# A convolution, attention and LoRA-expert block: stores issued by ScalarE, residual sums fused on VectorE, one pass of the output projection, a new timetable of the side work

## The reference

```python
x = x + layernorm(attn(layernorm(x)))
x = x + layernorm(ffn(layernorm(x)))
# attn: convolution over tokens, 3 taps, 1024 -> 768 (+ bias), split into q, k, v of 256;
#   wq, wk, wv to 16 heads of 64 (+ biases); blocks of 128 tokens: causal softmax(q k / 8) v;
#   wo back to 256 (+ bo); proj_w 256 -> 1024 (+ proj_b)
# ffn: logits = x Wr^T over 4 experts, the best 2, softmax of those as gates;
#   delta = sum_e gate_e * (x A_e^T) B_e^T * 4, rank 16
```

## Time and profile before

| | |
|---|---|
| median of 3 runs | 935.11 us (932.56 to 935.26) |
| the profiled execution, its own time | 938.93 us |
| its span, first to last instruction | 937.1 us |
| mean granted TensorE clock | 0.914 |
| TensorE / VectorE / ScalarE / GpSimd busy | 769.7 / 632.5 / 414.0 / 405.9 us |
| moved by DMA | 160.64 MB |

### The profile page before, as it was taken

How to read it: one execution, slowest core, us unless ns; L and a number is a source line. 1 busy time by engine, 2 the same in 40 slices (tenths; PEclk the granted TensorE clock), 3 DMA queues, 4 the chain that set the end, 5 groups by cost and what they waited for, 6 DMA issues and landing times.

```text
span 937.1 us, 14761 instructions
## 1 busy us (share of the span) xinstructions
PE 769.7 (82%) x5136; PEld 683.4 (73%) x5136; DVE 632.5 (67%) x1742; ACT 414.0 (44%) x1000; POOL 405.9 (43%) x348
## 2 busy tenths in 40 slices
PE   2489858999789788999879788999878877997573
PEld 1488757788679677888779776888778876876472
DVE  5999945995586545986496555886486551655846
ACT  3453345775335325675125325675135323454232
POOL 2566663575564441465164451455164450121111
PEclk9979988999989888999898988999898989999856
DMA  7267793334955475313944565312944444425102
GB/s 216 71 217 237 283 347 138 131 116 137 336 202 203 135 280 197 108 58 115 365 160 169 169 249 205 129 51 99 383 168 169 158 157 170 135 81 185 38 1 90
DMA packets 106361, 160.64 MB, mean 171 GB/s; under 512 B 7600, under 2 KB 76208, under 8 KB 106288
## 3 DMA queue, kind: packets, MB, share of 16 engines
q1 hardware_dynamic: 106288, 159.70, 49.0%
HBM read 128.22 MB, written 31.46 MB: 170 GB/s over the span
## 4 chain that ended last, share of the span: by engine, by line
PE 47%; DVE 28%; DMA 8%; ACT 5%; issue 5%; POOL 4%; SPq 2%; ACTq 0%; DVEq 0%; POOLq 0%
PE bank L763 11%; PE bank L764 10%; PE bank L765 10%; DMA w_pair<-kept_pairs 5%; PE bank L859 4%; PE bank L840 4%; PE bank L897 3%; PE bank L848 2%; ACT prob L1013 2%; DVE stats L1317 2%; PE bank L890 2%; DVE newton L1099 2%; DVE newton L1100 2%; POOL work L1399 2%; DVE ln_r L1097 2%
## 5 line engine op out<-in xcount | busy, mean ns | idle before, releaser
L763 PE MATMUL bank<-f_hi,w_pair 128*128 128x256 f32 x768 | 228.0, 297 | 25.7 <-DVE w_pair L1168 7.3
L764 PE MATMUL bank<-f_lo,w_pair 128*128 128x256 f32 x768 | 222.3, 290 | 0.0
L765 PE MATMUL bank<-f_hi,w_pair 128*128 128x256 f32 x768 | 221.8, 289 | 0.0
L1373 POOL TENSOR_TENSOR w_pair<-raw,w_pair 128x512 fp32r<-128x512 f32 (+1 forms) x115 | 148.7, 1306 | 126.9 <-ACT w_pair L963 126.9
L763 PEld LDWEIGHTS bank<-f_hi,w_pair 128*128 128x128 f32 x768 | 152.8, 199 | 31.4 <-DVE f_lo L1134 8.3
L1384 POOL TENSOR_TENSOR prob<-prob,rtotal 128x512 f32<-128x512 f32 x64 | 84.5, 1332 | 195.1 <-DVE rtotal L1223 195.1
L764 PEld LDWEIGHTS bank<-f_lo,w_pair 128*128 128x128 f32 x768 | 152.9, 199 | 0.9
L765 PEld LDWEIGHTS bank<-f_hi,w_pair 128*128 128x128 f32 x768 | 152.3, 198 | 0.0
L1013 ACT ACTIVATE prob<-prob,ntop 128x128 f32<-128x128 f32 x256 | 99.3, 391 | 51.2 <-DVE ntop L1219 51.1
L963 ACT ACTIVATE w_pair<-raw 128x512 fp32r<-128x512 f32 (+1 forms) x124 | 73.1, 610 | 72.0 <-PE bank L765 45.5
L1380 POOL TENSOR_TENSOR k_t<-q_t 128x256 f32<-128x256 f32 x48 | 37.7, 805 | 56.4 <-ACT q_t L980 50.7
(11 more groups left out here) (132 smaller groups left out, 1738.2 us busy)
## 6 DMA issues: line engine op xcount, KB each, us to landing
w_pair<-kept_pairs SPq DMA_DIRECT2D x132, 512.0 KB, 4.3
raw<-conv_w SPq DMA_DIRECT2D x96, 256.0 KB, 4.1
kept_pairs<-w_pair SPq DMA_DIRECT2D x40, 512.0 KB, 5.1
work<-x SPq DMA_DIRECT2D x32, 512.0 KB, 6.4
out<-work SPq DMA_DIRECT2D x16, 512.0 KB, 2.8
w_pair<-kept_pairs SPq DMA_DIRECT2D x24, 256.0 KB, 3.0
v<-conv_w SPq DMA_DIRECT2D x12, 256.0 KB, 3.3
kept_pairs<-w_pair SPq DMA_DIRECT2D x8, 256.0 KB, 3.2
```

What stands on the lines that cost most here:

```text
L763: pe.matmul(dst, w_h, m_h, start=start, stop=False)
L764: pe.matmul(dst, w_h, m_l, start=False, stop=False)
L765: return pe.matmul(dst, w_l, m_h, start=False, stop=stop)
L1373: pool.tensor_tensor(lo, raw_of(k)[:, 0:n], hi.bitcast(F32), ALU.subtract).then_inc(*split_low_pool.now(k))
```

## The change

- SyncE no longer issues `keep` and `store`; ScalarE does. A piece is now kept when the use of two pieces before it comes (`KEEP_LEAD` = 2), no longer right behind its split.
- `add_norm2`: one VectorE instruction, work = y * r + work; the shift of the mean is left out there, since ln3 doesn't see it, and is added to that of ln4 by one further instruction in `std`. `out_scale`: VectorE adds the scaled PSUM halves into `work`, then ScalarE adds the shift in place. Both GpSimd stages go.
- `project_out`: one call for four tiles and both halves; the four pieces are freed at the fourth tile. The list of pieces has 4 for it per batch instead of 8.
- The tables `SIDE` and `TAIL` are new. Statistics of the last two tiles of the next x and `std` of ln1 now stand right ahead of `scale_x`.
- The value copies wait for `lora_turn` instead of the final sum; the last residual loads wait for the stores.

```diff
-LEAD = 5
+LEAD, KEEP_LEAD = 5, 2
...
 SIDE = [
-    (9, "project_out", 0, 0), (9, "project_out", 0, 1), (10, "project_out", 2, 0), (11, "add_norm2", 0), (11, "project_out", 2, 1),
-    (16, "add_norm2", 2), (16, "norm3", 0), (20, "lora_turn", 0), (23, "norm3", 2), (23, "lora_mid", 0),
-    (23, "lora_turn", 1), (25, "lora_mid", 1), (26, "lora_turn", 2), (28, "gates", 0), (28, "lora_mid", 2),
-    (29, "lora_turn", 3), (30, "turn_mid", 0), (31, "lora_mid", 3), (33, "lora_out", 0), (35, "gates", 2),
-    (37, "turn_mid", 2), (38, "lora_out", 2), (38, "next_x", 0), (38, "next_x", 1), (43, "next_x", 2),
-    (44, "next_stats", 0), (44, "next_stats", 1), (44, "next_x", 3), (46, "next_stats", 2),
+    (9, "project_out"), (10, "add_norm2", 0), (12, "add_norm2", 2), (14, "norm3", 0), (18, "norm3", 2),
+    (24, "lora_turn", 0), (25, "lora_mid", 0), (26, "lora_turn", 1), (27, "lora_mid", 1), (29, "gates", 0),
+    (30, "lora_turn", 2), (31, "lora_mid", 2), (32, "lora_turn", 3), (33, "lora_mid", 3), (35, "turn_mid", 0),
+    (35, "gates", 2), (36, "lora_out", 0), (41, "turn_mid", 2), (42, "lora_out", 2),
+    (44, "next_x", 0), (44, "next_x", 1), (47, "next_x", 2), (47, "next_x", 3), (47, "next_stats", 0), (47, "next_stats", 1),
 ]
 TAIL = [
-    ("project_out", 0, 0), ("project_out", 0, 1), ("add_norm2", 0), ("project_out", 2, 0, "stream", 0), ("tick",),
-    ("norm3", 0, 3), ("project_out", 2, 1, "turn", 2), ("tick",), ("tick",), ("tick",), ("lora_turn", 0), ("lora_mid", 0),
-    ("add_norm2", 2), ("tick",), ("lora_turn", 1), ("norm3", 2, 2), ("tick",), ("lora_mid", 1), ("tick",), ("gates", 0),
+    ("project_out", ("side", "side", "stream", "stream")), ("add_norm2", 0), ("tick",), ("norm3", 0, 1), ("add_norm2", 2), ("tick",),
+    ("norm3", 2, 1), ("lora_turn", 0), ("lora_mid", 0), ("tick",), ("lora_turn", 1), ("lora_mid", 1), ("tick",), ("gates", 0),
     ("lora_turn", 2), ("lora_mid", 2), ("lora_turn", 3), ("lora_mid", 3), ("tick",), ("turn_mid", 0), ("gates", 2),
...
     def use_chunk(self, *name, over=True):
         k = NUMBER[name]
         self.split_chunks(k + LEAD)
+        while self.kept < len(KEEP) and KEEP[self.kept] <= k + KEEP_LEAD:
+            self.put("keep", KEEP[self.kept])
+            self.kept += 1
...
-    def project_out(self, b, t0, n, kind="side", lag=0):
-        for t in (t0, t0 + 1):
-            self.take(("project_out", b, t, n), kind, "attn_out", b, t, n)
-            for kt in range(KW):
-                self.use_chunk("proj", b, t0, n, kt, over=t > t0)
+    def project_out(self, b, kinds=("side",) * TB):
+        for t, kind in enumerate(kinds):
+            for n in range(2):
+                self.take(("project_out", b, t, n), kind, "attn_out", b, t, n)
+                for kt in range(KW):
+                    self.use_chunk("proj", b, n, kt, over=t == TB - 1)
...
                 if i == 0 and more:
+                    for t in (TB - 2, TB - 1):
+                        put("x_stats", b + 1, t)
+                    self.std("ln1", b + 1, 0, TB)
                     for t in range(TB):
                         put("scale_x", b + 1, t)
...
             def out_scale(b, t0):
+                _, _, nmr = norms["ln4"]
                 for t in (t0, t0 + 1):
...
+                    w.wait_ge(*ln4_added(b, t, 1))
+                    act.activation(work[t][:, :], work[t][:, :], ACT.Identity, bias=nmr[:, t:t + 1]).then_inc(*moe_done.now(b, t))
+
+            def store(b, t0):
+                for t in (t0, t0 + 1):
+                    w.wait_ge(*moe_done(b, t))
+                    act.dma_start(out[b * TB + t], work[t][:, :]).then_inc(s_out[t], 16)
...
+                if norm == "ln4":
+                    link(ins)
+                    ins = dve.tensor_tensor(nmr[:, ts], nmr[:, ts], norms["ln2"][2][:, ts], ALU.add)
...
             def add_norm2(b, t0):
+                _, rr, _ = norms["ln2"]
+                w.wait_ge(*std_done("ln2", b, t0))
                 for t in (t0, t0 + 1):
-                    if adds_on_dve(b, t):
-                        w.wait_ge(*work_full("residual", b, t))
-                        w.wait_ge(*ln2_done(b, t))
-                        dve.tensor_tensor(work[t][:, :], work[t][:, :], y[t], ALU.add).then_inc(*x1_dve.now(b, t))
+                    w.wait_ge(*work_full("residual", b, t))
+                    dve.scalar_tensor_tensor(out=work[t][:, :], in0=y[t], scalar=rr[:, t:t + 1], in1=work[t][:, :],
+                                             op0=ALU.mult, op1=ALU.add).then_inc(*x1_done.now(b, t))
...
             def out_scale(b, t0):
+                    for j in range(2):
+                        kind, i, _ = plan.bank["lora_out", b, t, j]
+                        half = work[t][:, j * 512:(j + 1) * 512]
+                        dve.scalar_tensor_tensor(out=half, in0=banks_of[kind][i][:, :], scalar=rr[:, t:t + 1], in1=half,
+                                                 op0=ALU.mult, op1=ALU.add).then_inc(*ln4_added.now(b, t, j))
```

More of the change, by code:

```diff
@@ L94, in conv_names @@
                 if stage == "project_out":
-                    names.extend(("proj",) + args + (kt,) for kt in range(KW))
+                    names.extend(("proj", b - 1, n, kt) for n in range(2) for kt in range(KW))
     done = 0
@@ L111, in chunk_names @@
                 done += FILL[i]
-    for stage, *args in TAIL:
-        if stage == "project_out":
-            names.extend(("proj", NB - 1, *args[:2], kt) for kt in range(KW))
+    names.extend(("proj", NB - 1, n, kt) for n in range(2) for kt in range(KW))
     return names
@@ L400, in make @@
                 self.project_v(b, 0, t)
-                if more and t == 3:
-                    put("x_stats", b + 1, TB - 1)
-                    self.std("ln1", b + 1, 0, TB)
             self.settle()
@@ L674, in build @@
         attn_out = Signal(sem("attn_out"), at("proj_bias"))
-        x1_dve = Signal(sem("x1_dve"), [s for s in pairs("add_norm2") if adds_on_dve(*s)])
+        x1_done = Signal(sem("x1_done"), pairs("add_norm2"))
         logits_out = Signal(sem("logits_out"), at("mid_out"))
@@ L690, in build @@
         prob_full = Signal(sem("prob_full"), at("normalise"))
-        x1_pool = Signal(sem("x1_pool"), [s for s in pairs("add_norm2") if not adds_on_dve(*s)])
-        moe_pool = Signal(sem("moe_pool"), [s for s in pairs("out_scale") if not adds_on_dve(*s)])
         s_raw = [sem(f"s_raw{i}") for i in range(RAW_SLOTS)]
@@ L1028, in finish_wo @@
                     act.activation(po_hi[:, m, :], wo_banks[m][:, :], ACT.Identity, bias=out_bias(m)).then_inc(*po_high.now(b, m))
-            def add_norm2(b, t0):
-                for t in (t0, t0 + 1):
-                    scale_row("ln2", b, t0, t, y[t], y[t]).then_inc(*ln2_done.now(b, t))
             def scale3(b, t0):
@@ L1057, in out_scale, with keep @@
             def out_scale(b, t0):
+                _, _, nmr = norms["ln4"]
                 for t in (t0, t0 + 1):
-                    for j in range(2):
-                        kind, i, _ = plan.bank["lora_out", b, t, j]
-                        scale_row("ln4", b, t0, t, y[t][:, j * 512:(j + 1) * 512], banks_of[kind][i][:, :]).then_inc(*ln4_done.now(b, t, j))
+                    w.wait_ge(*ln4_added(b, t, 1))
[4 more added lines that the diff above has]
+                    act.dma_start(out[b * TB + t], work[t][:, :]).then_inc(s_out[t], 16)
+            def keep(k):
+                i, n = k % SPLIT_SLOTS, width_of(k)
+                w.wait_ge(*split_high(k))
+                w.wait_ge(*split_low(k))
+                act.dma_start(kept_pairs[KEPT_AT[weights_of(CHUNKS[k])], :, :, 0:n], w_pair[i][:, :, 0:n].bitcast(F32)).then_inc(s_kept[i], 16)
             run = {
@@ L1488, in setup @@
                         sp.dma_start(half[rows, :], b_t[:, i * 512:(i + 1) * 512]).then_inc(s_lora, 16)
-            def store(b, t0):
-                for t in (t0, t0 + 1):
-                    w.wait_ge(*moe_done(b, t))
-                    sp.dma_start(out[b * TB + t], work[t][:, :]).then_inc(s_out[t], 16)
             run = {
-                "load": load, "bring": bring, "keep": keep, "load_tap1": load_tap1, "load_x": load_x, "load_residual": load_residual,
-                "setup": setup, "store": store,
+                "load": load, "bring": bring, "load_tap1": load_tap1, "load_x": load_x, "load_residual": load_residual,
+                "setup": setup,
             }
```

71 lines of the change are left out of this document (23 added, 48 removed).

## The result

| | before | after |
|---|---|---|
| median, us | 935.11 (932.56 to 937.62) | 943.72 (940.45 to 946.07) |
| ratio | | 1.0091 (95% interval 1.0058 to 1.0123) |
| the profiled execution, own time / span | 938.93 / 937.1 | 943.72 / 941.9 |
| mean granted clock | 0.914 | 0.916 |

What follows compares the result with a forecast made beforehand. TensorE was taken as busiest, with time to win or lose in three convolution stretches, seams and tail. Terms -16.5 + 6.6 - 4.2 + 4.3 + 1 + 3.5 = -5.3 us from 935.11 gave 930; range 902 to 942.

Steps and rivals of the forecast that it cites:

- The two holds: Convolution: ScalarE waits at scale3 ahead of weight splits, so TensorE idles about 8 us at slot 20, 4.5 at 24.
- (a): Output projection: TensorE's 2.20 us wait for weights goes with its clock loss, -4.6 us a block.
- (c): Transposition of the gated middle: TensorE's 6.97 us wait for VectorE goes, with 1.8 us of clock loss.
- the last seam: Behind the last convolution, with no next x: wait of 4.08 us falls to 1.7, with 1.8 of clock, -4.2 us.
- (d): Value projection: 4.08 us wait for weights behind a store goes with stores off SyncE; 1.7 us idle in its place.
- VectorE becomes the bound: Rival, chance 0.20: each of four sums meets a GpSimd split and costs 2.3 us, 13 us in three blocks; 943.
- Conv stretches: Three convolution stretches with the previous batch's side work: less idle time and clock loss, -5.5 us each, -16.5 in all.
- 17.2 us behind the pass: VectorE's chain behind the output projection: ln3 of the first pair is done 17.2 us after the pass ends.
- Second and third seam: From value projection to transposition of next x: late stores and statistics cost +3.3 us each, +6.6 together.
- First seam: First value projection to x transposition: 5.3 us later exponentials and 2 of clock, less 3 from earlier loads, +4.3 us.
- Tail: End of the kernel: first transposition 3 us later, eight fused sums in a row, one wait less; +3.5 us (-3 to +6).
- One hold instead of two: Rival, chance 0.30: second pair's ln3 is ready before ScalarE reaches slot 19, so the slot 24 stall goes; 905.

Runs made afterwards that it cites:

- the old slots: The changed kernel in all its parts, but with the SIDE table's side work at the slots of before the change: 909.58 us, 0.9709 of the kernel before.
- the run with the later loads: Against the table before it: next x loaded at slots 43, 43, 47, 47 instead of 41, 41, 44, 44, next_stats at 47 instead of 46; 896.48 us, 0.9577.
- the table before it: Changed kernel with sums ahead of statistics, later scale3, earlier gates, turn_mid, lora_out, next x and its statistics: 895.32 us, 0.9562 of the kernel before.

## Why the prediction was wrong

**The pieces that held.** The two holds were forecast by place, cause and size (8.2 and 4.5; 9.26 and 5.10 in the third block, though only 4.55 and 4.42 in the second batch's stretch). The ends of (a) and (c) came as forecast, and so did the last seam (-4.2, -4.5) and the 3 us to the tail's first transposition (21.3 to 24.2 us behind the projection's start). That (d) ended was forecast too, but not rightly why: with the stores back on SyncE it stayed away as well. *VectorE becomes the bound* gave 943, and 943.72 was measured; that is luck, for its mechanism did not occur. With GpSimd held, the sums took 1.24 us, which was its own "against". Where GpSimd works they do meet it, two take 3.5 instead of 2.5 us in the old slots; that is the rule of the Trainium skill (SBUF — State Buffer, Who interferes with whom), and c_lo and the step of `std` above agree with it.

**The step that failed** is the sum: four of its terms (conv stretches, later seams, first seam, tail) were each sized 2 to 4 us too favourably, in an effect of five. From -5.3 to +4.8 are 10.1 us:
- *Conv stretches*, -16.5 forecast, -12.1 measured: 4.4. "17.2 us behind the pass" was 19.1, because I priced the chain undisturbed right behind the pass, where GpSimd still had three splits to do. In the second batch's stretch (a) was not gone either: the wait for a pair from DRAM fell from 6.90 to 3.10 us.
- *Second and third seam*, +6.6 forecast, +5.0 in the seams and +3.6 in the attention behind them: 2.0. The gap was 8.3 and 9.5 us, not 7.0, by the late load; and I had counted its clock in the first seam alone. The row above shows the grant at 0.69 behind the gap of 9.53, where before it was 1.00.
- *First seam*, +4.3 forecast, +6.3 and +1.4 measured, less 1.1 gained ahead of it: 2.3. "These loads go out some 3 us earlier" failed: they went out 0.3 to 2.2 us earlier (the third piece of wk in this stretch at 131.68, before 132.75), and TensorE itself arrived 1.1 us earlier; the wait for value copies is 10.16 us, before 9.30. SyncE's keeps are not what held them, as the wait is 10.65 with the keeps back on SyncE. SyncE had to wait for raw places that GpSimd had yet to free; the longest of these waits, 8.3 us, ended when the first load went out at 125.05. A piece of wk then took 6.1 us to land where it had taken 4.8 (medians, 124 to 133 us), with the DMA engines full in both traces (mean share 1.00 and 1.03 from 124 to 140 us). SyncE's waits from 124 to 140 us:

```profile
SPq L500 <- POOL w_pair L1376: 11.8, 3, 8.3
```

- *Tail*, +3.5 forecast, +6.3 measured, outside its own bounds: 2.8. "At the end eight fused sums follow each other" was counted, the stores behind four additions in ScalarE's order were not (2.8 us by the run with SyncE's stores). The copy behind `scale3` of the second pair was named, but what it brought, a new wait of 4.62 us, had no price of its own; a wait of 4.78 us that stood there before went. The pass alone, in its own order of the tail, cost 3.7 us there, about what was forecast for all.
- Against these, 1 us for the keeps, which nothing shows, and 0.3 of the last seam: 4.4 + 2.0 + 2.3 + 2.8 - 1.3 = 10.2.

The remaining 3.8 us of the 13.7 by which 930 fell short are the distance of the profiled execution from its median. The forecast set its -5.3 against the median, though it was worked out from a trace that stood 3.8 above it; with an effect of five us that was not small.

**The chance of faster**, 0.58, rested half on *One hold instead of two* (0.30). It needed a chain to ln3 that is shorter than my undisturbed prices gave, and the rows gave none; the chain was longer. What fewer holds are worth I had underrated too: 36 us with both `scale3` moved, which left one stall of 5.5 us in two blocks, where 25 was the price of a case without the second hold. With the first hold of 9.3 us gone, the stretches of the third and fourth batch were 10.3 and 11.2 us shorter. That fits a low clock behind it: the grant from 492.9 to 499.9 us of after is 0.73.

**What the change is worth.** Two of its parts are good, the sums (-24 us alone) and the pass (-13). The timetable gives back 36, the rest 9 net. Of the rest the stores on ScalarE cost 6 in after and the late statistics 5; the keeps' share stays open, and so does how far these add.

## What to carry to other kernels

In a program where each engine works through one list, the cost of an instruction is what stands behind its wait. `scale3` took 2.4 us and held ScalarE for 15.5, GpSimd for 17.1 and TensorE for 9.3, on data that TensorE did not need yet. Place a waiting instruction by when its input is ready, not by when its output is wanted, and try each part of a change in the old order as well: here that was the difference between -27 and +9 us. When a forecast is a small rest of terms that nearly cancel, and each may be off by some us, its sign is open, whatever its working.

## What was not expected of the hardware

- In the run with the later loads the granted clock was 0.892 over the span, against 0.938 for the table before it. In attention it stood at 0.95 where the other had 1.00, yet the second batch's took 83.4 us for 83.1, and both kernels 896. Over such a stretch 0.05 less grant cost far less than 5% here. Behind a gap it did cost its share: in the 10 us with 0.69 in the third seam of after TensorE did 46 matmuls, where the kernel before did 71 at 1.00. Why the two differ, no run shows. The stretch from 360 to 443 us, first with the later loads, then in the table before it:

```profile
360.00:443.00 83.00, 82.24 (x592) 71.36 (x591) 60.43 (x199) 49.89 (x154) 40.36 (x39) 0.95 0.35 116
```

```profile
360.00:443.00 83.00, 81.64 (x590) 70.90 (x591) 61.13 (x199) 50.03 (x155) 41.33 (x38) 1.00 0.35 115
```

- An instruction of two columns (one step of `std`) took 1.26 us instead of 0.16 beside a GpSimd split of 1.29 that had begun 0.04 us earlier, and both ended together: here it cost the rest of the other's time, however small the own work. The 2.35 us above is the same on a larger scale.
- ScalarE's queue issues transfers beside ScalarE's arithmetic. In the third seam of after (ScalarE and its queue) the issue of two stores began with the second addition:

```profile
560.99 1.15 ACT L1045 ACTIVATE work<-work,ln_nmr 128x1024 f32<-128x1024 f32 x1 [0.17 <-DVE work L1325]
561.00 1.51 ACTq L1050 DMA_DIRECT2D out<-work  x2
```

  So what stores on ScalarE cost here lies in their order and their landing; the issue took no time from the additions.
